# Moving the transposes of the odd head pair to the front of the even turn, in a fused attention kernel on one core

## What is computed

```python
q = jnp.einsum('qdh,bcd->bhcq', Q, x) * sq
k = jnp.einsum('qdh,bcd->bhcq', K, x) * sq
v = jnp.einsum('vdh,bcd->bhcv', V, x) * sv
att = jnp.einsum('bhcq,bhCq->bhcC', q, k) / d_query
att = jnp.where(causal, att, -jnp.inf)
p = jax.nn.softmax(att, axis=-1)
y = jnp.einsum('bhcC,bhCv->bhcv', p, v)
z = jnp.einsum('dvh,bhcv->bcd', W, y) * (math.sqrt(d_embed / d_value) / num_heads)
```

## Time and profile before

| | |
|---|---|
| time, median of 3 runs | 1300.69 us (1300.5 to 1302.07) |
| the profiled execution | 1301.22 us, of which 1299.5 us is the span of the trace |
| PE, PEld | 1234.2 us (95%), 1073.3 us (83%) |
| DVE, ACT, POOL | 1030.9 (79%), 1025.2 (79%), 588.2 us (45%) |
| mean granted TensorE clock | 0.992 |
| chain that ended last | PE 85%, DVE 5%, issue 3%, POOL 2%, ACT 2% |

### The profile page before, as it was taken

One profiled execution on the slowest core, in us unless ns is written; L12 is line 12 of the kernel. 1 busy time (PEld: TensorE's weight loads), 2 busy tenths in 40 slices (PEclk: granted clock), 3 DMA queues, 4 the chain that ended last, 5 costly groups with the idle time before them and its releaser, 6 DMA issues.

```text
span 1299.5 us, 39139 instructions
## 1 busy us (share of the span) xinstructions
PE 1234.2 (95%) x11395; PEld 1073.3 (83%) x11395; DVE 1030.9 (79%) x4814; ACT 1025.2 (79%) x3426; POOL 588.2 (45%) x913
## 2 busy tenths in 40 slices
PE   5799977899999999999999999999999999999996
PEld 4688966778888888888888888888888888888885
DVE  6888879877778787878787887878787877787774
ACT  4866657578888888888888888888888888888883
POOL 4722247534444444444444444444444444444443
PEclk9999989999999999999999999999999999999999
DMA  8000000000000000000000000000000000000000
GB/s 216 1 2 0 1 2 1 1 2 2 3 10 0 8 1 8 0 8 0 8 0 8 0 8 0 8 0 8 0 8 0 8 0 8 0 8 0 9 2 18
DMA packets 14445, 11.83 MB, mean 9 GB/s; under 512 B 852, under 2 KB 12664, under 8 KB 14200
## 3 DMA queue, kind: packets, MB, share of 16 engines
q1 hardware_dynamic: 14240, 11.19, 3.2%
q10 hardware_dynamic: 152, 0.00, 0.0%
HBM read 7.00 MB, written 4.19 MB: 9 GB/s over the span
## 4 chain that ended last, share of the span: by engine, by line
PE 85%; DVE 5%; issue 3%; POOL 2%; ACT 2%; DMA 1%; SPq 1%; DVEq 0%; POOLq 0%; ACTq 0%
PE ps L1110 16%; PE ps L1141 14%; PE ps L1124 12%; PE ps L1150 9%; PE ps L1095 6%; PE ps L1096 5%; PE ps L1097 4%; PE ps L1132 2%; PE ps L1131 2%; PE ps L1130 2%; PE ps L973 1%; PE ps L995 1%; PE ps L1072 1%; PE ps L1051 1%; POOL rstd L318 1%
## 5 line engine op out<-in xcount | busy, mean ns | idle before, releaser
L797 ACT ACTIVATE pr<-ps,neg_max 128x128 f32<-128x128 f32 (+1 forms) x1024 | 426.2, 432 | 119.5 <-DVE neg_max L536 119.5
L333 POOL TENSOR_TENSOR pr<-pr,rinv 128x256 f32<-128x256 f32 x256 | 157.7, 616 | 555.0 <-DVE rinv L544 555.0
L536 DVE CUSTOM_DVE_ANT_0 ps<-ps,mask 128x128 f32<-128x128 f32 (+1 forms) x1024 | 329.1, 388 | 3.4
L335 POOL TENSOR_TENSOR pr<-pr,rinv 128x512 f32<-128x512 f32 x256 | 266.6, 1041 | 0.0
L551 DVE COPY pT<-ps 128x512 f32<-128x512 f32 x256 | 175.3, 685 | 100.1 <-PE ps L1124 100.1
L797 ACT ACTIVATION_READ_ACCUMULATOR pr<-ps,neg_max 128x1 f32 x1024 | 219.1, 214 | 0.0
L1124 PE MATMUL ps<-ident,pr 128*128 128x128 f32 x1536 | 210.2, 273 | 3.8 <-DVE pT L551 1.9
L1124 PEld LDWEIGHTS ps<-ident,pr 128*128 128x128 f32 x1536 | 179.1, 141 | 23.0 <-POOL pr L335 4.3
L1141 PE MATMUL ps<-pT,space 128*64 128x256 f32 (+1 forms) x2048 | 194.9, 332 | 0.7 <-ACT pT L806 0.5
L1141 PEld LDWEIGHTS ps<-pT,space 128*64 128x64 f32 x2048 | 126.8, 136 | 55.0 <-ACT pT L806 0.7
L1095 PE MATMUL ps<-x_hi,wqk_hi 128*128 128x256 f32 x512 | 168.5, 329 | 0.4 <-ACT qk_raw L770 0.3
(11 more groups left out here) (182 smaller groups left out, 2640.7 us busy)
## 6 DMA issues: line engine op xcount, KB each, us to landing
out<-x_all SPq DMA_DIRECT2D x16, 256.0 KB, 2.3
x_all<-L_attn_x SPq DMA_DIRECT2D x1, 768.0 KB, 6.7
x_all<-L_attn_x SPq DMA_DIRECT2D x1, 512.0 KB, 4.6
space<-L_attn_Q SPq DMA_DIRECT2D x1, 512.0 KB, 15.6
space<-L_attn_K SPq DMA_DIRECT2D x1, 512.0 KB, 9.6
space<-L_attn_V SPq DMA_DIRECT2D x1, 512.0 KB, 11.5
space<-L_attn_W SPq DMA_DIRECT2D x1, 512.0 KB, 12.1
dft_s<-dft SPq DMA_DIRECT2D x1, 192.0 KB, 2.6
```

What stands on the lines that cost most here:

```text
L333: nc.gpsimd.tensor_tensor(pr[:, buf, :, 0, :], pr[:, buf, :, 0, :], r[:, :, 0:1].to_broadcast([P, 2, P]), ALU.mult)
L335: nc.gpsimd.tensor_tensor(pr[:, buf, :, 1:3, :].rearrange("p h b k -> p h (b k)"), pr[:, buf, :, 1:3, :].rearrange("p h b k -> p h (b k)") ...
L536: last = nc.vector.tensor_tensor_reduce(o, o, mask[:, T - w:T], -1.0, -MASKED, ALU.add, ALU.min, neg_max[:, j, 2 * h + qt:2 * h + qt + 1])
L797: last = nc.scalar.activation(dst, ps[:, BANK_S + 2 * j + h, qt * P:qt * P + w], ACT.Exp, bias=neg_max[:, j, at:at + 1], scale=-1.0, accum ...
```

## The change

The function is cut into two, with a semaphore each. In an even turn the four blocks for `BANK_T` now go ahead of `qk_product`, directly behind the last turn's `products`, and the two for `BANK_Y` directly behind `qk_product`, ahead of the extra piece. Odd turns keep their order. DVE copies the odd pair's four blocks right behind the first `inv_sum`. The order on ACT stays, with other semaphores to wait for.

```diff
             def probs_T(n, j):
 
-                dve.wait_ge(pt_done, count(n + 1))
+                dve.wait_ge(pta_done, count(n + 1))
...
                     inv_sum(n, 0)
+                    if not (first and p == 0):
+                        probs_T(n - 1, 1)
                     if p == 0 and above_0(b - 1):
                         z_norm(b - 2)
...
-                    if not (first and p == 0):
-                        probs_T(n - 1, 1)
                     if not (last and p == PAIRS - 2):
                         qk_low(n + 2, 0)
...
                     if above_0(kept):
-                        act.wait_ge(pt_done, count(kept))
+                        act.wait_ge(ptb_done, count(kept))
...
             def probs_T(n, j):
 
-                act.wait_ge(pt_done, count(n + 1))
+                act.wait_ge(ptb_done, count(n + 1))
...
-            def probs_transpose(n, j, buf, y_calls):
+            def probs_transpose_a(n, j, buf):
                 pe.wait_ge(pn_ready, count(n + 1))
                 if above_0(n):
                     pe.wait_ge(pTa_ready, count(n))
-                for k in range(6):
-                    if k == 4 and above_0(n):
-                        pe.wait_ge(pTb_ready, count(n))
-                        pe.wait_ge(y_ready, count(y_calls))
-                    to = ps[:, BANK_T, k * P:(k + 1) * P] if k < 4 else ps[:, BANK_Y, j * T + (k - 4) * P:j * T + (k - 3) * P]
-                    last = tr(to, pr[:, buf, k // 3, k % 3, :], ident[:])
-                last.then_inc(pt_done, 1)
+                for k in range(4):
+                    last = tr(ps[:, BANK_T, k * P:(k + 1) * P], pr[:, buf, k // 3, k % 3, :], ident[:])
+                last.then_inc(pta_done, 1)
+
+            def probs_transpose_b(n, j, buf, y_calls):
+                if above_0(n):
+                    pe.wait_ge(pTb_ready, count(n))
+                    pe.wait_ge(y_ready, count(y_calls))
+                for k in range(2):
+                    last = tr(ps[:, BANK_Y, j * T + k * P:j * T + (k + 1) * P], pr[:, buf, 1, k + 1, :], ident[:])
+                last.then_inc(ptb_done, 1)
...
                     n, j = b * PAIRS + p, p % 2
+                    if p % 2 == 0 and not (first and p == 0):
+                        probs_transpose_a(n - 1, 1 - j, pr_of(p - 1))
                     if not (last and p >= PAIRS - 2):
...
                         qk_product(n + 2, (p + 2) % PAIRS, jb if p + 2 < PAIRS else 1 - jb, j)
+                    if p % 2 == 0 and not (first and p == 0):
+                        probs_transpose_b(n - 1, 1 - j, pr_of(p - 1), b * (PAIRS // 2) + p // 2)
...
-                    if not (first and p == 0):
-                        probs_transpose(n - 1, 1 - j, pr_of(p - 1), b * (PAIRS // 2) + p // 2)
+                    if p % 2 == 1:
+                        probs_transpose_a(n - 1, 1 - j, pr_of(p - 1))
+                        probs_transpose_b(n - 1, 1 - j, pr_of(p - 1), b * (PAIRS // 2) + p // 2)
```

More of the change, by code:

```diff
@@ L201, in build @@
         s_done = sem("s_done"); max_ready = sem("max_ready"); exp_ready = sem("exp_ready")
-        rinv_ready = sem("rinv_ready"); pn_ready = sem("pn_ready"); pt_done = sem("pt_done")
+        rinv_ready = sem("rinv_ready"); pn_ready = sem("pn_ready"); pta_done = sem("pta_done"); ptb_done = sem("ptb_done")
         pTa_ready = sem("pTa_ready"); pTb_ready = sem("pTb_ready")
@@ L1243, in _ @@
             spectral_transpose(B - 2)
-            probs_transpose(B * PAIRS - 1, 1, pr_of(PAIRS - 1), B * PAIRS // 2)
+            probs_transpose_a(B * PAIRS - 1, 1, pr_of(PAIRS - 1))
+            probs_transpose_b(B * PAIRS - 1, 1, pr_of(PAIRS - 1), B * PAIRS // 2)
             pe.wait_ge(z_xT_ready, B - 1)
```

## The result

The changed kernel takes 1356.85 us (median of 4 runs, 1355.37 to 1358.05) against 1301.03 us of the kernel before (4 runs, 1300.5 to 1302.07). The ratio is 1.0426, with a 95% interval of 1.0412 to 1.044: 4.3% slower, 55.8 us. Forecast were 1361.1 us and 60.4 us.

What follows compares the result with a forecast made beforehand. PE, 99.9% busy, was taken to wait in a chain through ACT, at its limit though 83% busy. 62 x 0.67 + 30 x 0.63 = 60.4 us on 1300.7 us gave 1361.1 us, range 1341 to 1376 us.

Steps and rivals of the forecast that it cites:

- ACT's inputs come later: Even turns: PE's projection comes 0.44 us later and the extra piece 0.67 us later, and ACT wants both at once.
- Pair 6: Turn pair 6, 31 batches: values end later, ACT's 3.50 us chain follows unchanged, odd scores start later; plus 0.67 us each.
- Pair 0: Turn pair 0, 31 batches: built like turn pair 6, with a quarter of the values in both turns; plus 0.67 us each.
- Pair 2: Turn pair 2, 30 batches: late transposes of z delay `x_high`, `x_low` and turn 3's output projection; plus 0.63 us each.
- Pair 4: Turn pair 4: ACT's copy of the projection comes 0.44 us later, but a 0.42 us gap takes it up; 0 us.
- rival A: Only the values' turn pairs pay, as turn 3's output projection isn't held by `x_low`; 41.5 us, 1342 us; chance 0.08.
- Where PE waits: Sign: turn pairs 6 and 0, PE waits most of 0.67 us more between the even and odd pair's scores.
- The copy of the two blocks "waits for nothing": Inside ACT's 3.50 us chain in turn pair 6, this copy was said to wait for nothing, leaving the chain unchanged.
- The bounded costs: Taken as 0: `pn_ready` wait on POOL behind the products (6 us if late), `y_ready` wait, 256 semaphore increments (skill: 6.7 us).
- B, a lower clock: Rival: PE's waits in the attention make its granted clock fall about five times, adding 7 to 15 us; chance 0.07.
- C, faster: Rival: DVE's earlier copy in turn pairs 6 and 0 removes PE's wait ahead of the odd scores; 1284.4 us; chance 0.06.
- D, no difference: Rival: the delay on ACT and the earlier transposes cancel within 2.6 us; 1300.7 us; chance 0.04.

## Why the prediction was right

**ACT's inputs come later: right.** The chain was read from ends and starts 0.03 to 0.04 us apart in the kernel before, and it is the chain that the after shows: PE projection, PE values, ACT without a break, odd scores. These start 698.60 - 692.73 = 5.87 us behind the turn pair's start, before 710.66 - 705.41 = 5.25 us, 0.62 us later. Work added to ACT there costs its full length, 0.5 us a time; of 0.5 us taken off 0.23 us is gained, which is all that PE waited there. In turn pair 4 added work costs next to nothing; taking work off there was not tried.

**The later of the two inputs decides: right.** With the projection on time and the values late the loss is the same.

**Turn pair by turn pair.** Pair 6: forecast 0.67 us, measured 0.61 us. Pair 0: 0.67 and 0.59 us. Pair 2: 0.63 us for the start of the output projection, measured 3.29 - 2.66 = 0.63 us. Pair 4: nothing, and measured 8.74 - 8.70 = 0.04 us less. A whole batch takes 726.38 - 692.73 = 33.65 us, before 720.66 - 688.80 = 31.86 us, 1.8 us more where 2.0 us were forecast. Pair 2 alone costs 19.7 us, which ends rival A.

**Where PE waits: not as forecast.** A sign of being right was to be that PE waits for most of 0.67 us more between the even and the odd pair's scores. It waits there 0.94 - 0.91 = 0.03 us more, and 0.59 us more ahead of the even pair's scores. The forecast had followed only one of the two places at which PE depends on the same ACT queue, the last head's exponential ahead of the odd scores. The earlier one is ACT's copy of the odd pair's two blocks, which PE needs before it can transpose the even pair's two. Both move with ACT's late start, so the delay of the turn pair comes out the same.

**The size: 60.4 us forecast, 55.8 us measured, 4.6 us less.** The term that was mis-sized is what six transposes put ahead of the values cost PE, 0.67 us. The values' last matmul starts 694.63 - 692.73 = 1.90 us behind the turn pair's start, before 706.69 - 705.41 = 1.28 us: 0.62 us. I had assumed that the change of operands behind the products costs a transpose as much as it costs the projection. The first of four transposes there makes the row 0.06 us longer than that of four elsewhere (0.66 against 0.60 us), the first projection matmul there has a row 0.11 us longer than the others (0.39 against 0.28 us). With 0.60 us, the mean of what turn pairs 6 and 0 lost, 62 x (0.67 - 0.60) is 4.3 us, nearly all of the difference. The 0.62 us are read directly from starts; that the switch of operand kinds explains them is read from few rows, and the first projection matmul behind transposes has a long row too (0.37 us). The prediction had named this term as its uncertainty downwards, with about 5 us.

**The copy of the two blocks "waits for nothing": true, but incomplete.** ACT's copy waits for nothing, but PE waits for it, 59 times in the attention. By the rows this is not a further cost in the changed kernel: the odd pair's scores start 0.06 us behind the end of ACT's head, and would have to wait for it if PE had reached them earlier. No run takes this wait away alone, so that is argued and not shown.

**The bounded costs.** POOL's slack behind the products held: from the start of the products to the next turn pair it is 700.93 - 699.48 = 1.45 us, before 713.00 - 711.55 = 1.45 us. The reason given for it was wrong in part. POOL does not follow from the same exponential as the odd scores, which ended at 710.62, but from `inv_sum`, which stood in DVE's queue until 711.03; that queue waits for ACT as well, and so moved with it. The semaphores were free.

**The rivals.** B, a lower clock: the window above has 1.00, so has every window of 20 us from 320 to 1340 us in the changed kernel, and the mean over the span is 0.993 against 0.992. Neither the short waits of PE, busy for 117 of 120 us, nor the four transposes behind the products lowered it. C, faster: DVE's order alone is slower. The wait of 0.23 us ahead of the odd scores could be gained in turn pair 6, but through ACT's queue and not through DVE's place for the copy. D, no difference: the measured 4.3% rules it out.

## What to carry to other kernels

When a block is moved forward in an in-order queue, cost what it is moved past, by who consumes that: here 0.6 us of work that nobody awaited was put ahead of results for which another engine stood ready within 0.04 us (0.08 us in turn pair 2). The idle time that it took away (100 us on DVE) was worth nothing, as the next thing in that queue waited for the same late engine. To find such a place before a change, compare the end of each producer with the start of its consumer; a copy of dummy data on the suspected engine, in one place and then in another, tests it for the price of two runs. Where the test cost time here, moving a copy to the engine with the idle gap gained 0.6%.

The wait itself shows, as here, at the first place where the queue depends on the late engine, and that need not be the place from which the chain was read.

## What was not expected of the hardware

What follows the products (weight loads of 64 columns, two matmuls at a time) seems to pay for the switch, and not every kind the same: by the rows' lengths 0.06 us for a transpose and 0.11 us for the projection's matmul. No run measured this by itself. Over the 92 places of the forecast the difference of 0.05 us makes 4.6 us.
